# From the fifth block on, three quarters of the second layer in high and low parts, read from the PSUM banks, and the table of late blocks made earlier

## The chip, the cores and the metric

The kernel runs on one core of one Trainium2 chip, in one launch. The metric is device time in microseconds (us) of that core, the median of several executions. TensorE is called PE here, VectorE DVE, ScalarE ACT, GpSimd POOL and SyncE SP.

## The reference

```python
x = x + cross_attention(ctx_1024, layernorm(x))     # 32 batches, 128 context and 128 latent rows, 16 heads of 64
x = x + ffn(layernorm(x))

def ffn(x):                                          # 4096 tokens, E = 8 experts, D = 256, F = 1024
    assign = argmax(x @ centroids.T, axis=1)         # one expert for each token
    xn = normalise(x) * ln_g[e] + ln_b[e]
    h  = relu(xn @ w1[e].T + b1[e])                  # first layer, 256 -> 1024
    y  = x + h @ w2[e].T + b2[e]                     # second layer, 1024 -> 256
    a  = sigmoid(x @ centroids[e])
    return a * y + (1 - a) * x
```

Everything is float32 at the interface.

## The kernel before, in words

**Attention first, then blocks.** The first three quarters of the program are the attention: 64 steps over 16 pairs of batches. Each batch's finished rows are scattered by POOL into a table in HBM, `sorted_rows`, by expert. The feed-forward works on that table in blocks ("slots") of 256 rows of one expert. There are at most 23 slots; which expert and which rows a slot has is computed on DVE and read by SP as a register. The first six (`n_early` = 6) are placed before the last batches are ranked, by `early_blocks`; the others by `late_blocks` (line 1600), which also computes how many slots stay empty. From slot 16 on each engine branches around slots that are empty. In this input slots 0 to 18 run.

**Numbers in two parts.** PE multiplies plain float32 in two recorded passes, and the reduced format fp32r in one. To keep the accuracy with fp32r a number is split: `hi` is the number rounded to fp32r, `lo` the rest, and a product is made of three matmuls, `PASSES = ((0, 0), (0, 1), (1, 0))` (line 31). The first layer of slots 1 and up is wholly in parts (`layer_1`, line 888, matmuls on line 902). The second layer has 8 chunks of 128 hidden units (`FC` = 8). Of these `FS` = 4 go in parts (`in_parts`, line 929, matmuls on line 932) and 4 plain (`plain`, line 936, matmuls on line 938), for each of the two halves of 128 rows.

**One slot, engine by engine.** PE runs `layer_1(s + 1)`, then `layer_2_split(s)`. The first layer fills PSUM banks 0 to 3, two chunks each.

- ACT: `relu_parts(s + 1)` (line 1226) reads each bank and writes the first four chunks to `hid_raw` in SBUF (the tile `y_t`) and the last four to `hid_plain` (the tile `prob_t`); then `row_gain_bias(s + 2)` (1190, instruction 1208), `high_weights_2(s + 1)` (1244, instruction 1251), and at the head of the next slot `normalise_rows` (1172, instruction 1186) and `high_weights_1` (1164, instruction 1170).
- DVE: `low_weights_1(s + 2)` (instruction 1635), `split_hidden(s + 1)` (1638, instructions 1644 and 1645, once for each bank of two chunks in parts), `split_xn(s + 2)` (1622, instructions 1629 and 1631), `transpose_rows(s + 3)` (instruction 1620), `finish(s)` (1647, instructions 1658 and 1663 twice). `then_next` (1362) makes the next DVE instruction wait for a semaphore that the one before raises.
- POOL: `add_base(s + 2)` (two of instruction 1891), `low_weights_2(s + 1)` (1895, one instruction on line 1898 over 1024 elements), `write_rows(s)` (1903), an indirect DMA for each half.
- SP: the loads of the slots to come, in an order written out by hand (lines 652 to 670): `load_vectors`, `load_rows`, `load_weights_1`, `load_weights_2`, `load_b2`, and `move_rows`.

**What waits for what.** `layer_1(s)` waits for `f_xd` (`split_xn(s)` done), for `f_wl` (`low_weights_1(s)` done), and for each bank `i` until ACT has read it out two slots before (`f_ha`, line 894). `layer_2_split(s)` waits for `f_w2h`, `f_w2l` (the parts of its weights) and `f_hl` (the parts of its hidden units). The tiles of the feed-forward lie over tiles of the attention: `hid_hi` over `v_n`, `hid_lo` over `prob`, `w2_hl` in `head_out` and `w_o`.

**The hand-over.** Around slots 1 to 5 the order is written out line by line. On DVE (lines 1766 to 1791) it ends with `places` of the last two batches, `low_weights_1(4)`, `split_hidden(3)`, `split_xn(4)`, `late_blocks()`, `finish(2)`. On SP (lines 652 to 665) `load_weights_2(5)` and `load_b2(5)` come before the wait for the table and the first loads of slots 6 and 7.

## Time and profile before

| | |
|---|---|
| median of 3 runs | 1053.27 us (1052.5 to 1053.7) |
| the profiled execution | 1052.73 us |
| its span | 1050.9 us |
| granted clock of PE | 0.999 |
| PE busy | 1041.6 us, 99% |
| DVE, ACT, POOL busy | 844.9, 688.7 and 565.3 us |
| the feed-forward slots | from about 800 us to the end |

The span runs from the first recorded instruction to the last; the rest of the profiled time, 1.8 us, lies around it. All times of instructions are counted from the span's start. The chain is the sequence of work that ended last, followed back from the last instruction; a piece of it is counted from the end of the piece before.

### The profile page before, as it was taken

The page shows a single profiled execution, that of the slowest core. Times are in us where ns is not written, and L with a number is a line of the kernel's source. Part 1 is how long each engine was busy: PE and PEld are TensorE (multiplying, and loading weights), DVE is VectorE, ACT ScalarE, POOL GpSimd, SP SyncE. Part 2 cuts the span into 40 slices and gives each one's busy share as a digit, 9 for nine tenths or more (in the row PEclk, how much of TensorE's full clock was granted, in tenths as well). Part 3 has the DMA queues.
Part 4 walks back from the last instruction along what each step waited for, and adds up shares of the span by engine and source line. Part 5 has one row for each costly group of instructions (what it writes and reads, how often), then busy time and mean ns, then how long its engine had stood idle before and what let it go on. Part 6 is the DMA issues. An engine that isn't in the chain of part 4 may idle for free.

```text
span 1050.9 us, 24670 instructions
## 1 busy us (share of the span) xinstructions
PE 1041.6 (99%) x8610; PEld 940.5 (89%) x8610; DVE 844.9 (80%) x1979; ACT 688.7 (66%) x1838; POOL 565.3 (54%) x665
## 2 busy tenths in 40 slices
PE   9999999999999999999999999999999999999997
PEld 7889898988888888889898989889888999999997
DVE  7878888878888888888888879888887797767663
ACT  6765757675666767666757575766566666676761
POOL 1744464646454555545464646465444667566663
PEclk9999999999999999999999999999999999999999
DMA  6665657585757576767667585856356868777760
GB/s 212 160 169 148 170 156 189 146 215 142 201 146 197 142 193 155 200 156 197 159 168 185 142 210 137 213 144 171 91 153 196 307 198 294 250 234 234 249 194 31
DMA packets 159666, 190.57 MB, mean 181 GB/s; under 512 B 17454, under 2 KB 149038, under 8 KB 154673
## 3 DMA queue, kind: packets, MB, share of 16 engines
q1 hardware_dynamic: 155088, 179.09, 62.4%
q0 software_dynamic: 3360, 8.53, 2.2%
q8 instruction: 72, 1.18, 0.4%
q10 hardware_dynamic: 1088, 1.31, 0.4%
q14 instruction: 58, 0.47, 0.1%
HBM read 65.72 MB, written 46.07 MB: 106 GB/s over the span
## 4 chain that ended last, share of the span: by engine, by line
PE 96%; DVE 2%; POOL 1%; ACT 1%; DMA 0%; issue 0%; POOLq 0%; DVEq 0%
PE psum L742 17%; PE psum L775 16%; PE psum L812 11%; PE psum L902 10%; PE psum L791 10%; PE psum L827 9%; PE psum L761 8%; PE psum L938 6%; PE psum L932 5%; PE psum L830 1%; PE psum L883 1%; PE psum L914 1%; DVE neg_max L1410 1%; DMA c_in<-in_ctx_in 0%; PE psum L856 0%; DVE w_lo L1545 0%
## 5 line engine op out<-in xcount | busy, mean ns | idle before, releaser
L1823 POOL TENSOR_TENSOR prob<-prob,inv_sum 128x512 f32<-128x512 f32 x172 | 177.7, 1047 | 190.1 <-DVE inv_sum L1416 189.2
L1133 ACT ACTIVATE prob<-psum,neg_max 128x256 f32<-128x256 f32 x344 | 160.2, 478 | 38.8 <-DVE neg_max L1410 38.5
L1410 DVE TENSOR_REDUCE neg_max<-psum 128x2 f32<-128x512 f32 x256 | 161.9, 672 | 27.7 <-PE psum L791 27.5
L1422 DVE STREAM_TRANSPOSE prob<-prob 128x512 f32<-128x512 f32 x172 | 118.5, 698 | 12.3 <-POOL prob L1823 11.9
L1823 POOL TENSOR_TENSOR w_ring<-w_ring,inv_sum 128x512 f32<-128x512 f32 x76 | 78.1, 1041 | 76.0 <-DVE inv_sum L1416 75.7
L1140 ACT ACTIVATE head_out_hi<-psum 128x512 fp32r<-128x512 f32 x52 | 31.1, 597 | 105.6 <-PE psum L812 102.4
L1119 ACT ACTIVATE v_n<-psum 128x512 f32<-128x512 f32 x128 | 77.9, 608 | 26.7 <-PE psum L775 22.7
L1108 ACT ACTIVATE k_hi<-psum 128x512 fp32r<-128x512 f32 x128 | 77.0, 603 | 22.0 <-PE psum L742 21.3
L1461 DVE TENSOR_TENSOR k_lo<-psum,k_hi 128x512 fp32r<-128x512 f32 x128 | 85.7, 674 | 0.0
L742 PE MATMUL psum<-kv_t_hi,w_hi 128*128 128x512 f32 x252 | 85.0, 419 | 0.0
L775 PE MATMUL psum<-w_hi,kv_t_hi 128*128 128x512 f32 x256 | 80.2, 395 | 0.4 <-DVE k_lo L1461 0.4
L1133 ACT ACTIVATE w_ring<-psum,neg_max 128x256 f32<-128x256 f32 x152 | 70.7, 477 | 14.6 <-DVE neg_max L1410 14.6
L791 PE MATMUL psum<-k_hi,q_hi 64*128 64x256 f32 x512 | 79.1, 305 | 0.8 <-DVE q_lo L1468 0.7
L775 PE MATMUL psum<-w_lo,kv_t_hi 128*128 128x512 f32 x256 | 79.4, 391 | 0.0
L775 PE MATMUL psum<-w_hi,kv_t_lo 128*128 128x512 f32 x256 | 79.3, 391 | 0.0
L742 PE MATMUL psum<-kv_t_lo,w_hi 128*128 128x512 f32 x252 | 78.1, 391 | 0.0
L742 PE MATMUL psum<-kv_t_hi,w_lo 128*128 128x512 f32 x252 | 77.9, 390 | 0.0
L1133 ACT ACTIVATION_READ_ACCUMULATOR prob<-psum,neg_max 128x1 f32 x344 | 72.5, 211 | 0.0
L791 PE MATMUL psum<-k_lo,q_hi 64*128 64x256 f32 x512 | 72.5, 279 | 0.0
L791 PE MATMUL psum<-k_hi,q_lo 64*128 64x256 f32 x512 | 72.3, 278 | 0.0
L938 PE MATMUL psum<-w,prob_t 128*128 128x256 f32 x288 | 65.3, 379 | 0.0
L812 PE MATMUL psum<-w_ring,v_n 128*64 128x128 f32 x1024 | 63.0, 276 | 0.3 <-DVE cent_sum L1501 0.3
(215 smaller groups left out, 2952.4 us busy)
## 6 DMA issues: line engine op xcount, KB each, us to landing
sorted_rows<-filler SPq DMA_DIRECT2D x54, 660.0 KB
prob_t<-prob SPq DMA_DIRECT2D x172, 128.0 KB, 2.8
w_ring<-prob SPq DMA_DIRECT2D x172, 128.0 KB, 2.7
w<-in_experts SPq DMA_DIRECT2D x19, 1024.0 KB, 7.8
w_ring<-in_experts SPq DMA_DIRECT2D x18, 1024.0 KB, 6.7
prob_t<-w_ring SPq DMA_DIRECT2D x76, 128.0 KB, 2.8
w_ring<-w_ring SPq DMA_DIRECT2D x76, 128.0 KB, 2.7
w_ring<-normed SPq DMA_DIRECT2D x56, 128.0 KB, 3.0
```

Source lines behind the costliest of these rows:

```text
L742: last = pe.matmul(bank.rearrange("p (b t) -> p b t", b=2), k_w[hw][:, c, col:col + P], kv_t[hx][:, c, slot:slot + 2, :], start=(n == 0 an ...
L775: last = pe.matmul(bank, kv_t[hx][:, c, slot, side * P:(side + 1) * P], v_w[hw][:, c, col:col + BANK], start=(n == 0 and c == 0), stop=(n ...
L791: ins = pe.matmul(psum[:, 2 * bb + parity, i * 2 * P:(i + 1) * 2 * P], q_s[hq][rows, u % 2, i, bb * P:(bb + 1) * P], k_s[hk][rows, u % 2, ...
L812: last = pe.matmul(bank[rows, (2 * bb + i) * P:(2 * bb + i + 1) * P].rearrange("p (a q) -> p a q", a=4), v_n[:, h % 2, bb, side, head * DH ...
L827: pe.matmul(bank[:, 0:d_model + n_experts], heads, w_o[hw][:, c, :], start=(n == 0 and c == 0), stop=False)
L902: last = pe.matmul(dst, w1_hl[hw][s % NW][:, c, f * P:(f + 1) * P], xn_hl[hx][:, s % 2, c, :], start=(n == 0 and c == 0), stop=(n == 2 and ...
L938: last = pe.matmul(bank, hid_plain[:, s % 2, f - FS, i * P:(i + 1) * P], w2_ring[s % NW2][:, f * d_model:(f + 1) * d_model], start=(first ...
L1133: act.activation(prob_at(u, bb)[:, :, parity, i], scores_i, ACT.Exp, bias=neg_max[:, at, i:i + 1], accum_out=prob_sum[:, at, i:i + 1]).the ...
L1410: dve.tensor_reduce(neg_max[:, (4 * u + n) % 8, :], psum[:, n, :].rearrange("p (i j) -> p i j", i=2), AXIS_X, ALU.max, negate=True).then_i ...
L1422: dve.transpose(probs, probs).then_inc(s_quad, 1)
L1461: last_reads(item, dve.tensor_tensor(k_s[1][:, u % 2, i, :], work_bank(number[item]), k_s[0][:, u % 2, i, :], ALU.subtract))
L1823: pool.tensor_tensor(probs, probs, inverse, ALU.mult).then_inc(s_soft, 1)
```

## The change

From slot 4 (`FIRST_MORE`) on, the second layer takes 6 of its 8 chunks in parts and 2 plain; slots 1 to 3 stay at 4 and 4. For these slots ACT writes the ReLU of the chunks back to the PSUM bank that it read (`hidden_raw`), and DVE splits it out of the bank, three banks for a slot. `layer_1` therefore waits for banks 0 to 2 until DVE has split them (`f_hl`), for bank 3 still for ACT. ACT no longer waits for `f_hl` in these slots. `hid_hi` and `hid_lo` get 8 chunks for each of two slots (over `v_n`, and over `prob` and `prob_t`), and the plain chunks now lie in the place of `hid_hi` that belongs to their number. ACT's `high_weights_2` covers 1536 elements in place of 1024, and POOL's `low_weights_2` becomes three instructions of 512 elements. On DVE `late_blocks()` goes ahead of `low_weights_1(4)`, and `split_xn(4)` ahead of `split_hidden(3)`. On SP `load_weights_2(5)` and `load_b2(5)` go behind the wait for the table, the rows and vectors of slot 6, the rows of slot 7 and the first-layer weights of slot 6.

```diff
+FIRST_MORE = 4
-            FS = FC // 2
+            SPLIT_EARLY, SPLIT = FC // 2, 3 * FC // 4
-                hid_hi = sbuf(late, "hid_hi", [P, 2, FS, BLOCK], F32R)
-                sbuf(late, "hid_between", [P, 3 * FS * BLOCK])
-                hid_lo = sbuf(late, "hid_lo", [P, 2, FS, BLOCK], F32R)
+                hid_hi = sbuf(late, "hid_hi", [P, 2, FC, BLOCK], F32R)
+                sbuf(late, "hid_between", [P, FC // 2 * BLOCK])
+                hid_lo = sbuf(late, "hid_lo", [P, 2, FC, BLOCK], F32R)
+            def hidden_raw(s, i):
+                return psum[:, i, :] if s >= FIRST_MORE else hid_raw[:, i, :]
+            def n_split(s):
+                return SPLIT if s >= FIRST_MORE else SPLIT_EARLY
+            def hidden_split(s):
+                return sum(n_split(t) // 2 for t in range(FIRST_SPLIT, s + 1))
 # SP
-                load_weights_2(n_early - 1)
-                load_b2(n_early - 1)
                 scattered(n_batches)
                 run = block_steps(sp, count_empty(sp))
                 run(n_early, (load_rows,), (load_vectors,))
                 run(n_early + 1, (load_rows,))
                 run(n_early, (load_weights_1,))
+                load_weights_2(n_early - 1)
+                load_b2(n_early - 1)
                 run(n_early + 1, (load_weights_1,))
 # PE, layer_1
+                        elif s > FIRST_MORE and i < SPLIT // 2:
+                            pe.wait_ge(f_hl, hidden_split(s - 2) + i + 1)
                         else:
                             pe.wait_ge(f_ha, FC // 2 * (s - 2) + i + 1)
 # PE, layer_2_split
-                        pe.wait_ge(f_hl, FS // 2 * (s - FIRST_SPLIT + 1))
+                        pe.wait_ge(f_hl, hidden_split(s))
-                            for f in range(FS):
+                            for f in range(split):
-                        for f in range(FS, FC):
+                        for f in range(split, FC):
 # ACT, relu_parts
-                        if i < FS // 2 and s > FIRST_SPLIT:
-                            act.wait_ge(f_hl, FS // 2 * (s - 1 - FIRST_SPLIT) + i + 1)
-                        elif i == FS // 2 and s >= 2:
+                        if i < split // 2 and FIRST_SPLIT < s < FIRST_MORE:
+                            act.wait_ge(f_hl, hidden_split(s - 1) - SPLIT_EARLY // 2 + i + 1)
+                        elif i == split // 2 and s >= 2:
                             wait_made(act, ("fy", s - 2, 1))
-                            dst = hid_raw[:, i, at] if f < FS else hid_plain[:, s % 2, f - FS, :]
+                            dst = hid_plain[:, s % 2, f - SPLIT_EARLY, :] if f >= split else hidden_raw(s, i)[:, at]
 # DVE
                 def split_hidden(s):
-                    for i in range(FS // 2):
+                    for i in range(n_split(s) // 2):
 ...
-                        then_next(dve.tensor_copy(hi, hid_raw[:, i, :]))
-                        dve.tensor_tensor(lo, hid_raw[:, i, :], hi, ALU.subtract).then_inc(f_hl, 1)
+                        raw = hidden_raw(s, i)
+                        then_next(dve.tensor_copy(hi, raw))
+                        dve.tensor_tensor(lo, raw, hi, ALU.subtract).then_inc(f_hl, 1)
 ...
                 places(n_batches - 1)
+                late_blocks()
                 low_weights_1(4)
+                split_xn(4)
                 split_hidden(3)
-                split_xn(4)
-                late_blocks()
                 finish(2)
 # POOL
                 def low_weights_2(s):
                     pool.wait_ge(f_w2h, s - FIRST_SPLIT + 1)
-                    raw = w2_ring[s % NW2][:, 0:FS * d_model].rearrange("p (f d) -> p f d", f=FS)
-                    pool.tensor_tensor(w2_hl[s % 2][1], raw, w2_hl[s % 2][0], ALU.subtract).then_inc(f_w2l, 1)
+                    raw = w2_ring[s % NW2][:].rearrange("p (f d) -> p f d", f=FC)
+                    hi, lo = w2_hl[s % 2]
+                    piece = 2 if s >= FIRST_MORE else SPLIT_EARLY
+                    for f in range(0, n_split(s), piece):
+                        last = pool.tensor_tensor(lo[:, f:f + piece], raw[:, f:f + piece], hi[:, f:f + piece], ALU.subtract)
+                    last.then_inc(f_w2l, 1)
```

## Rows read from the trace of the kernel before

**Rows 1.** The page, part 4: the chain that ended last, by engine.
```profile
PE 96%; DVE 2%; POOL 1%; ACT 1%; DMA 0%; issue 0%; POOLq 0%; DVEq 0%
```

**Rows 2.** The chain in order of time: start us, us, what, instructions.
```profile
857.15 5.76 PE psum L902 x48
...
869.66 5.76 PE psum L902 x48
...
876.86 3.46 PE psum L938 x16
...
881.75 5.76 PE psum L902 x48
...
1032.55 1.44 PE psum L932 x12
```

**Rows 3.** Lines 938 and 902 alone: count, durations ns min/median/max, first and last start us.
```profile
L938 PE MATMUL psum<-w,prob_t x288: 376/379/382, 837.5 to 1043.4; 128*128 128x256 f32 x144
L902 PE MATMUL psum<-k_hi,w_hi x288: 282/283/386, 818.3 to 1031.8; 128*128 128x256 f32 x144
```

**Rows 4.** Timeline of one late slot: start us, us, engine, line, [idle before].
```profile
931.00 2.28 DVE L1635 TENSOR_TENSOR w_lo<-w_ring,w_hi 128x2048 fp32r<-128x2048 f32 x1
...
937.61 1.05 ACT L1251 ACTIVATE head_out_hi<-w 128x1024 fp32r<-128x1024 f32 x1
937.74 0.43 DVE L1629 CAST k_hi<-c_in 128x512 fp32r<-128x512 f32 x1 [1.91 <-ACT c_in L1208]
938.20 0.69 DVE L1631 TENSOR_TENSOR k_lo<-c_in,k_hi 128x512 fp32r<-128x512 f32 x1
...
938.74 2.40 POOL L1898 TENSOR_TENSOR head_out_lo<-w,head_out_hi 128x1024 fp32r<-128x1024 f32 x1 [2.48 <-ACT head_out_hi L1251]
...
940.18 0.71 DVE L1620 STREAM_TRANSPOSE normed<-normed 128x512 f32<-128x512 f32 x1 [1.29 <-ACT normed L1186]
...
943.66 0.84 ACT L1241 ACTIVATE y_t<-psum,vec_ring 128x256 f32<-128x256 f32 x2 [1.70 <-PE psum L902]
```

**Rows 5.** Groups and single lines that price the changed instructions.
```profile
L1461 DVE TENSOR_TENSOR k_lo<-psum,k_hi 128x512 fp32r<-128x512 f32 x128 | 85.7, 674 | 0.0
...
L1644 DVE CAST hid_hi<-y_t x36: 410/419/671, 825.6 to 1030.6; 128x512 fp32r<-128x512 f32 x36
...
L1881 POOL TENSOR_TENSOR w_o_lo<-w_ring,w_o_hi x4: 1282/1292/1299, 41.7 to 54.3; 128x512 fp32r<-128x512 f32 x4
```

**Rows 6.** Timeline: DVE instructions that start beside a POOL instruction, twice.
```profile
27.78 3.02 POOL L1823 TENSOR_TENSOR prob<-prob,inv_sum 128x512 f32<-128x512 f32 x2 [0.87 <-DVE inv_sum L1416]
...
28.27 1.62 DVE L1545 TENSOR_TENSOR w_lo<-r_ring,w_hi 128x1024 fp32r<-128x1024 f32 x1
...
843.17 2.36 POOL L1898 TENSOR_TENSOR head_out_lo<-w,head_out_hi 128x1024 fp32r<-128x1024 f32 x1 [2.91 <-ACT head_out_hi L1251]
843.37 2.45 DVE L1663 SCALAR_TENSOR_TENSOR x_in<-x_in,r_ring,base 128x256 f32<-128x256 f32 x1
```

**Rows 7.** Timeline of the hand-over: the table of late blocks, and slot 5's preparation.
```profile
848.08 2.28 DVE L1635 TENSOR_TENSOR w_lo<-w_ring,w_hi 128x2048 fp32r<-128x2048 f32 x1
...
853.71 0.15 DVE L1561 COPY small<-psum 128x8 f32<-128x8 f32 x1
...
854.71 1.92 DVE L1604 TENSOR_TENSOR small<-small,taken 128x8 f32<-128x8 f32 x1
...
859.50 0.14 DVE L1614 CAST empty_i<-small 1x1 int32<-1x1 f32 x1
...
861.83 2.29 DVE L1635 TENSOR_TENSOR w_lo<-w_ring,w_hi 128x2048 fp32r<-128x2048 f32 x1
...
866.41 1.60 POOL L1891 TENSOR_SCALAR base<-r_more 128x256 f32<-128x256 f32 x2
```

**Rows 8.** Timeline of the last slot's weights.
```profile
1033.32 1.06 ACT L1251 ACTIVATE head_out_hi<-w 128x1024 fp32r<-128x1024 f32 x1
...
1034.46 2.35 POOL L1898 TENSOR_TENSOR head_out_lo<-w,head_out_hi 128x1024 fp32r<-128x1024 f32 x1 [4.90 <-ACT head_out_hi L1251]
```

More of the change, by code:

```diff
@@ L320, in build @@
             hid_raw = y_t[:].rearrange("p c b t -> p c (b t)")
-            hid_plain = prob_t_even[:].rearrange("p b a h i s q -> p b (a h i s q)").rearrange("p s (f t) -> p s f t", f=FC - FS)
-            w2_hl = [[w[:].rearrange(rule)[:, 0:FS * d_model].rearrange("p (f d) -> p f d", f=FS) for w in pair] for pair, rule in
+            hid_plain = v_n[:].rearrange("p s a b n -> p s (a b n)")[:, :, SPLIT_EARLY * BLOCK:].rearrange(
+                "p s (f t) -> p s f t", f=FC - SPLIT_EARLY)
+            w2_hl = [[w[:].rearrange(rule)[:, 0:FC * d_model].rearrange("p (f d) -> p f d", f=FC) for w in pair] for pair, rule in
                      ((head_out, "p b c t -> p (b c t)"), (w_o, "p c n -> p (c n)"))]
@@ L919, in layer_2_split @@
                 def layer_2_split(s):
+                    split = n_split(s)
                     pe.wait_ge(f_w2[s % NW2], 16 * (s // NW2 + 1))
@@ L926, in wait_parts, with in_parts @@
                         pe.wait_ge(f_w2l, s - FIRST_SPLIT + 1)
-                        pe.wait_ge(f_hl, FS // 2 * (s - FIRST_SPLIT + 1))
-                    def in_parts(bank, i, first):
+                        pe.wait_ge(f_hl, hidden_split(s))
+                    def in_parts(bank, i, first, last):
                         for n, (hw, hx) in enumerate(PASSES):
-                            for f in range(FS):
-                                last = pe.matmul(bank, hid_hl[hx][:, s % 2, f, i * P:(i + 1) * P], w2_hl[s % 2][hw][:, f, :],
-                                                 start=(first and n == 0 and f == 0), stop=(not first and n == 2 and f == FS - 1))
-                        return last
+                            for f in range(split):
+                                ins = pe.matmul(bank, hid_hl[hx][:, s % 2, f, i * P:(i + 1) * P], w2_hl[s % 2][hw][:, f, :],
+                                                start=(first and n == 0 and f == 0), stop=(last and n == 2 and f == split - 1))
+                        return ins
                     def plain(bank, i, first):
-                        for f in range(FS, FC):
-                            last = pe.matmul(bank, hid_plain[:, s % 2, f - FS, i * P:(i + 1) * P],
+                        for f in range(split, FC):
+                            last = pe.matmul(bank, hid_plain[:, s % 2, f - SPLIT_EARLY, i * P:(i + 1) * P],
                                              w2_ring[s % NW2][:, f * d_model:(f + 1) * d_model],
-                                             start=(first and f == FS), stop=(not first and f == FC - 1))
+                                             start=(first and f == split), stop=(not first and f == FC - 1))
                         return last
@@ L946, in layer_2_split @@
                         wait_parts(s)
-                        in_parts(bank, 0, False).then_inc(f_y, 1)
+                        in_parts(bank, 0, False, True).then_inc(f_y, 1)
                         bank = begin(("fy", s, 1))[:, 0:d_model]
-                        in_parts(bank, 1, True)
+                        in_parts(bank, 1, True, False)
                         plain(bank, 1, False).then_inc(f_y, 1)
@@ L952, in layer_2_split @@
                     wait_parts(s)
-                    in_parts(bank, 0, True)
+                    in_parts(bank, 0, True, False)
                     plain(bank, 0, False).then_inc(f_y, 1)
@@ L956, in layer_2_split @@
                     plain(bank, 1, True)
-                    in_parts(bank, 1, False).then_inc(f_y, 1)
+                    in_parts(bank, 1, False, True).then_inc(f_y, 1)
                 pe.wait_ge(s_blank, 1)
@@ L1226, in relu_parts @@
                 def relu_parts(s):
+                    split = n_split(s)
                     b1 = vec_ring[:, s % NR, 2 * KC:]
@@ L1250, in high_weights_2 @@
                         wait_made(act, ("fy", s - 2, 1))
[L1251 to L1252 removed]
+                    act.activation(w2_hl[s % 2][0][:, 0:n_split(s)], w2_ring[s % NW2][:, 0:n_split(s) * d_model]
+                                   .rearrange("p (f d) -> p f d", f=n_split(s)), ACT.Copy).then_inc(f_w2h, 1)
                 act.dma_start(c_in[:, 0:2, :], ctx_in[0:2].rearrange("b p d -> p b d")).then_inc(s_in[0], 16)
```

2 lines of the change are left out of this document (removed).

## The prediction, made before the changed kernel was run

> **What bounds the kernel now.** I read the chain first. 96% of it is PE [rows 1], so only two things can move the time: the work of PE itself, and a wait that comes to stand on it. Then the chain in order of time: from 857 us to the end it is one slot after another, and every start is the end of the one before. A slot is a first layer (48 matmuls, 5.76 us), a second layer in parts (two groups of 12), and between them the plain matmuls; from one first layer to the next it is 881.75 - 869.66 = 12.09 us [rows 2]. PE never waits there. Third I read the timeline of a late slot, to see how much room the other engines have [rows 4], and last the places where the order is not yet regular: the hand-over to the late slots [rows 7] and the last slot [rows 8].
>
> **The matmuls.** 16 plain records take 3.46 us, 0.216 each; 12 matmuls in parts take 1.44 us, 0.120 each [rows 2]. The change takes 8 plain records (1.73 us) out of a slot and puts in 12 in parts (2 halves, 2 chunks, 3 passes: 1.44 us). It saves 0.29 to 0.30 us. There are 16 plain records for each split slot and 288 in all [rows 3], so slots 1 to 18 run; 15 of them are from slot 4 on: 15 x 0.296 = **4.4 us saved**. A slot becomes 11.79 us long.
>
> **ACT.** The weights' high part grows from 1024 to 1536 elements: 1.05 us [rows 4] becomes at least 1.05 and in proportion 1.58; I take 1.5. ACT stands idle 1.70 us in each slot before its first ReLU [rows 4]; that hides it. If the cover were gone, 0.45 us a slot would delay the ReLUs, and next the splits. Writing the ReLU to PSUM in place of SBUF has no row. Nearest is the same ReLU to SBUF, 0.84 for two; it could be shorter or longer by some 0.1, also under that cover. I take it unchanged.
>
> **DVE.** Splitting out of the bank: the cast from SBUF takes 0.42 (an operand in SBUF, the same operation), a subtraction that reads 512 elements of PSUM 0.67 (the same source) [rows 5]. These are the bounds of the new cast; I take 0.67, because half the elements' time can hardly be lost by a subtraction that reads the same bank. The Trainium skill ("VectorE: DVE Perf Modes", section on why PSUM operands drop a tier) says that fp32 out of PSUM runs at the basic rate; by that rule it is the 0.67, and by the rate of the SBUF cast the sum would come out as in the first rival. A bank then costs 0.67 + 0.67 less the overlap, about 1.30 us, and a slot has three: 3.9 us where two took about 2.4.
>
> **POOL.** One subtraction of 1024 elements, 2.40 us [rows 4], becomes three of 512. POOL has done such a one: 1.29 us [rows 5]. So 3.9 us, 1.5 more.
>
> **Where POOL and DVE meet.** A DVE instruction with two operands in SBUF that starts beside POOL's subtraction does not run beside it: it ended 0.29 us behind it (843.37 + 2.45 against 843.17 + 2.36) [rows 6]. With two POOL instructions back to back DVE came between them: the pair took 3.02 us, and DVE's 1.62 ended at 29.89, before the second did at 30.80 [rows 6]. A transpose ran beside POOL undisturbed, 0.71 us [rows 4]. So a DVE step meets at most one piece each time it has to begin anew, 1.29 us. [...] The splits out of PSUM then wait for nothing, but the cast and the subtraction of `split_xn` do.
>
> **The regular slots.** Counted from the start of the first layer (929.9): DVE's low weights start at 1.1 now [rows 4]. `finish` of the slot before can meet up to two pieces, so 2.1 to 2.6; +2.2, +3.9: `split_xn` starts at 8.2 to 8.7 and ends 1.1 later, at the latest 9.9. It is due at 11.8. POOL's pieces start when ACT's weights are done, at 9.3, and end at 13.2; the second layer wants them at 17.5. PE's new wait for the bank: the third split is done at 8.7, the bank wanted at 14.7. Queued behind it on PE is the whole first layer, and the room is 6 us. **Nothing lost**, 1.9 us to spare.
>
> **The hand-over.** Here the room is less. The table took 853.71 to 859.64, 5.9 us, of which 1.75 was one small subtraction held up by POOL [rows 7]. Moved up it starts at 848.1 and ends at 852.3; `low_weights_1(4)` (2.28) ends at 854.6, `split_xn(4)` (1.15) at 855.7. The first layer of slot 4 is counted from 857.15 and must be released some 0.3 earlier, one matmul's 0.28 [rows 2, 3]: just in time. If POOL's 2.4 us subtraction for slot 3 falls in the gap of `split_xn(4)`, it ends at 858.1, and PE loses 1.2. `split_hidden(3)` and `finish(2)` follow, and `low_weights_1(5)` starts where it did, 861.83. The splits of slot 4 start at 864.0 and end at 867.9; there `split_xn(5)` now starts. POOL ends `add_base(5)` at 868.0 [rows 7], or up to 0.4 earlier, as less is in its way, and starts its three pieces: they collide. If the cast waits for the first piece and the subtraction for the second: 868.0 + 1.29 + 0.4 + 1.29 + 0.55 = 871.5. Due is 869.4 (869.66 less 0.3 [rows 2, 3]): 2.1 late. If the cast gets ahead and only the subtraction waits, 870.2: 0.8 late. If neither meets a piece, 869.0: nothing. Together the hand-over costs 0 to 2.5 us; I take **1.7**. What comes after is later by as much, and slot 6 has room again. The moved loads on SP: the rows and first weights of slot 6 are issued some 5 us sooner (seven issues with their register loads), `load_weights_2(5)` and `load_b2(5)` a few us later; their users come 15 us after. I cost them at nothing; without the cover it would be one load, some 7 us.
>
> **The end.** The last slot has no first layer behind it. Its second layer is due 6.03 us after 1032.55, less 0.3, on the clock of before at 1038.3. ACT's weights end at 1033.32 + 1.5 = 1034.8, POOL's three pieces at 1038.7, and with one `finish` between them at 1039.1 [rows 8, 5]. PE waits 0.4 to 0.9 us; I take **0.8**. Ends: nothing, and 1.5 if every piece meets DVE.
>
> **The sum.** -4.4 + 1.7 + 0.8 = -1.9 us. Against the profiled execution's own time, 1052.73, that is 1050.8; it stands 0.5 below the median, so for the median 1053.27 - 1.9 = **1051.4**, say 1051.3. A measurement of this kernel can tell about 0.2%, 2.1 us, from no change: the forecast lies just within that. Its own range is -1.0 to -2.9, 1050.4 to 1052.3.
>
> **Rivals.**
> First, the collision at the hand-over doesn't happen: the cast out of PSUM is faster (at 0.42 the splits end 0.75 us sooner, ahead of POOL), or POOL starts later. For it: the two meet within 0.3 us. Against: 0.67 is the better price. Then -4.4 + 0 to 0.4 + 0.4 to 0.8: 1049.1 to 1050.1.
> Second, slower: DVE and POOL hold each other up in every late slot. The place is `split_xn`. If `finish` slips to 3.3 us after the start of the slot, the cast arrives when POOL's first piece has begun (9.4); it then waits until 10.7, the subtraction for the second piece until 12.3, and ends at 12.9 in place of 11.8: 1.1 us for each slot. That is the point from which it decides. In 13 slots 14 us: 1053.3 - 1.9 + 14 = 1065; in every third, 1056. For it: a cycle of DVE and POOL (three pieces, `finish`, 2.2, 3.9, 1.1) adds up to about 11.8, the length of the slot. Against: POOL's start hangs on ACT, not on DVE, so the cycle is not closed.
> Third, the change saves PE nothing, because what it saves in the second layer is waited for elsewhere in the slot. Every margin I find is above 1 us, against 0.3 saved. 1053.3.
>
> **The numbers.** Forecast 0.60: of this 0.22 is beyond 0.2% (below 1051.2), 0.38 within. First rival 0.25, all faster. Second 0.12: 0.10 slower, 0.02 within. Third 0.03, within. Faster 0.47, same 0.43, slower 0.10. The range reaches down to the first rival with the end's cost nearly gone, 1048.9, and up to 1054.5, where the hand-over and the end cost their most and one slot in five slips; left out are most of the second rival and a gain above 4.4.
>
> **What would show it.** Right: from slot 6 on the chain's period is 11.79 us, with two groups of 18 matmuls in parts and 8 plain records between; POOL's subtraction of 512 elements at 1.29; DVE's cast out of psum at 0.67; a gap of 0 to 2 us on PE before the first layer of slot 4 or 5, released by DVE's `split_xn`, and one of 0.4 to 0.9 before the last second layer, released by POOL. Wrong: a period above 11.9 (second rival), no gap at the hand-over (first), a matmul in parts above 0.12 us, or ACT late with its first ReLU.

## The result, and the profile after

The changed kernel takes 1055.47 us (median of 21 executions, 1051.72 to 1057.99), the kernel before 1053.25 in the same comparison (1052.5 to 1055.03). The ratio is 1.0015, with a 95% interval of 1.0008 to 1.0022: 1.6 us slower, 0.8 to 2.3 (2.2 by the medians alone). The forecast was 1051.3, in a range up to 1054.5. The first thing to see is the spread: 6 us where the kernel before has 2.5. The second is that the loss is small beside it: a later set of 11 executions of the same kernel gave no loss ("The changed kernel again", below). So what follows explains why the forecast gain did not come; that the kernel is slower is less sure.

The profiled execution took 1055.55 us with a span of 1053.8, 2.9 above the span before. PE is busy less than before, 1038.5 us against 1041.6, so the saving is there, and more than all of it is lost in waits and what follows them. The page of after, parts 1 and 4:

```profile
PE 1038.5 (99%) x8670; PEld 940.0 (89%) x8670; DVE 876.5 (83%) x2009; ACT 694.0 (66%) x1838; POOL 582.0 (55%) x695
...
PE 93%; DVE 2%; POOL 2%; issue 1%; ACT 1%; DMA 0%; POOLq 0%; DVEq 0%; ACTq 0%
```

PE has fallen from 96% of the chain [rows 1] to 93%. What it waited for in the slots, from the waits of after (what ended the wait, us in total, times, longest):

```profile
PE psum L949 <- POOL w_o_lo L1921: 2.6, 1, 2.6
...
PE psum L918 <- issue: 1.0, 1, 1.0
...
PE psum L949 <- POOL head_out_lo L1921: 0.5, 1, 0.5
```

Lines 918, 949 and 955 are what 902, 932 and 938 were before: first layer, parts, plain. The chain of after in order of time (start us, us, what) puts these waits in their places:

```profile
857.09 1.05 issue
858.14 5.98 PE psum L918 x48
...
870.87 5.88 PE psum L918 x48
876.75 2.16 PE psum L949 x18
878.91 1.73 PE psum L955 x8
880.64 2.15 PE psum L949 x18
...
894.60 5.78 PE psum L918 x48
...
907.75 2.46 POOL base L1910
...
910.75 3.73 POOL w_o_lo L1921 x3
914.47 0.24 issue
914.72 2.95 PE psum L949 x18
917.66 2.77 PE psum L955 x8
920.44 2.15 PE psum L949 x18
922.58 5.76 PE psum L918 x48
...
934.38 5.76 PE psum L918 x48
...
1041.06 2.39 PE psum L949 x18
```

The regular slot is as forecast: 934.38 - 922.58 = 11.80 us, two groups of 18 in parts and 8 plain matmuls. Against it stand three places. The first layer of slot 4 is 1.05 us late: the moved `split_xn(4)` starts beside POOL's subtraction for slot 3, its cast (0.42 us alone) ends 0.28 us behind that subtraction, and the first layer starts when the rest of `split_xn(4)` is done at 858.04. The two lines, of POOL and of DVE:

```profile
853.16 3.87 POOL L1921 TENSOR_TENSOR w_o_lo<-w,w_o_hi 128x1024 fp32r<-128x1024 f32 x1 [0.54 <-ACT w_o_hi L1269]
854.70 2.61 DVE L1647 CAST k_hi<-c_in 128x512 fp32r<-128x512 f32 x1
```

The second layer of slot 7 was due at 912.2 (the first layer of slot 7 starts at 894.60; behind it come 5.78, a second layer of 6.04 and a first of 5.76) and starts at 914.72. The last second layer is some 0.5 late. And the matmuls behind the wait at slot 7 are slow: 2.95 where 2.16 is usual, 2.77 where 1.73 is. The stretches of after say why (stretch, its length, then busy time and count of PE, its weight loads, DVE, ACT and POOL, then PE's granted clock, the DMA engines' busy share and GB/s):

```profile
906.50:912.00 5.50, 5.50 (x48) 5.45 (x46) 5.39 (x8) 2.82 (x7) 4.25 (x4) 1.00 0.58 172
912.20:914.70 2.50, 0.00 (x0) 0.02 (x1) 2.19 (x4) 2.50 (x5) 2.26 (x2) 1.00 0.85 270
914.70:916.00 1.30, 1.28 (x11) 1.30 (x12) 0.74 (x2) 1.30 (x2) 0.63 (x1) 1.00 0.95 372
916.00:917.00 1.00, 1.00 (x8) 1.00 (x7) 0.12 (x1) 1.00 (x3) 0.69 (x2) 0.62 0.99 418
917.00:918.00 1.00, 1.00 (x6) 0.91 (x5) 0.59 (x1) 1.00 (x1) 0.96 (x2) 0.50 1.04 426
...
919.00:920.00 1.00, 1.00 (x4) 0.80 (x4) 0.42 (x1) 0.00 (x0) 1.00 (x2) 0.68 0.85 287
```

PE was fully busy, then idle for 2.5 us, and 1.3 us after it began again its clock went from 2.4 to 1.2 GHz for some 3 us. In this execution the wait is paid nearly twice.

The account of the profiled execution from the first layer of slot 4 to the end of the last second layer: -15 x 0.296 = -4.4 saved; slot 4 +1.05 and +0.3 for first layers of 5.98 and 5.88 in place of 5.76; slot 7 +2.5 of wait and +1.8 of half clock; the end +0.5 of wait and +0.2 in the matmuls behind it. Sum +2.0. PE's last matmul ends at 1047.35 where it ended at 1045.21 before: +2.1. The other 0.8 of the span lies behind PE's last matmul, at the last output write.

Why is POOL late at slot 7? Its timeline of after, then of before (start us, us, instruction, [idle before]):

```profile
898.58 2.32 POOL L1927 DMA_INDIRECT out<-x_in,r_more  x1 [0.30 <-issue]
907.75 3.00 POOL L1910 TENSOR_SCALAR base<-r_ring 128x256 f32<-128x256 f32 x2 [6.84 <-DVE x_in L1682]
910.72 3.75 POOL L1921 TENSOR_TENSOR w_o_lo<-w,w_o_hi 128x512 fp32r<-128x512 f32 x3
```

```profile
896.24 2.32 POOL L1903 DMA_INDIRECT out<-x_in,r_more  x1 [0.30 <-issue]
903.18 1.09 POOL L1891 TENSOR_SCALAR base<-r_ring 128x256 f32<-128x256 f32 x2 [4.62 <-issue]
904.23 2.41 POOL L1898 TENSOR_TENSOR w_o_lo<-w,w_o_hi 128x1024 fp32r<-128x1024 f32 x1
```

Between the output write of slot 5 and the first late slot POOL stands idle for 4.6 us before and 6.8 after. The code has two instructions there, ahead of the first `late_block`: a semaphore wait and a drain of POOL. I call the pair the entry wait. The semaphore wait (`f_out[0]` at 96) asks for the rows of slots 0, 2 and 4, the last of them slot 4's, and it costs nothing: the drain behind it is recorded from 0.16 us after the start of slot 5's second DMA instruction. The idle time is the drain's, in before and in after (count, its duration in ns, its start in us):

```profile
L1964 POOLq DRAIN  x1: 6592/6592/6592, 896.4 to 896.4; - x1
```

```profile
L1988 POOLq DRAIN  x1: 8817/8817/8817, 898.7 to 898.7; - x1
```

The profile names DVE's `finish` as what ended the idle time in after, because it ended at 907.59. But `add_base(8)`, the instruction behind the idle time, needs only `finish(4)`, and the drain's own record ends at 907.56. What the drain waits for can be read from the DMA packets in the traces. In all eleven profiled executions that have the entry wait it ends 2.1 to 2.2 us after the last packet of slot 5's write. That packet ends 4.5 us after the start of the second DMA instruction in before (at 900.78) and 6.8 us after it in after (905.35).

In before the entry wait ended in time for a single subtraction of 2.4 us, with the weights' low part ready at 906.6 against a due time of 911.7. In after the write is 2.3 us later (the three pieces for slot 6 and the `finish` that met them are ahead of it), the wait 2.2 longer, `add_base` meets DVE's `low_weights_1` (3.00 in place of 1.09), and the subtractions last 3.75: ready at 914.47. Of the 2.5 us that PE waits, that meeting is 1.9; without it, by the same numbers, PE would have waited an estimated 0.6.

### The profile page after: what moved, and what is told of

It reads as the page before. It is cut to its first block, busy times and chain, and to the rows that moved or that the text cites. A ratio compares the mean times of both kernels' runs of the same rounds, so it can differ in the third digit from the quotient of the medians.

```text
span 1053.8 us, 24820 instructions
## 1 busy us (share of the span) xinstructions
PE 1038.5 (99%) x8670; PEld 940.0 (89%) x8670; DVE 876.5 (83%) x2009; ACT 694.0 (66%) x1838; POOL 582.0 (55%) x695
## 4 chain that ended last, share of the span: by engine, by line
PE 93%; DVE 2%; POOL 2%; issue 1%; ACT 1%; DMA 0%; POOLq 0%; DVEq 0%; ACTq 0%
PE psum L756 17%; PE psum L789 16%; PE psum L826 11%; PE psum L805 9%; PE psum L841 9%; PE psum L918 9%; PE psum L775 8%; PE psum L949 6%; PE psum L955 3%; PE psum L844 1%; PE psum L897 1%; PE psum L930 1%; DVE neg_max L1428 1%; DMA c_in<-in_ctx_in 0%; POOL w_o_lo L1921 0%
## 5 line engine op out<-in xcount | busy, mean ns | idle before, releaser
L1259 ACT ACTIVATE psum<-psum,vec_ring 128x256 f32<-128x256 f32 x90 | 36.5, 444 | 44.7 <-PE psum L918 44.0
```

## The experiments

Theory A: the loss lies in the entry wait and what follows from it, beside 1.05 us at slot 4 and some 1 at the end. Rivals: the moved table or loads are at fault; or POOL and DVE hold each other up everywhere. Four sets of runs, with 8 to 12 executions of each kernel. Each set has its own runs of the kernel before, and the ratio is to those: 1053.85 us for the kernels again, without the entry wait, table back and parts from slot 8; 1053.46 for the kernel before without the entry wait, plain first, the two moves and the table in the middle; 1053.21 for both edits together, SP's order back, one instruction and parts from slot 6; 1053.04 for the last three. Kernels of different sets are compared by these ratios.

**The changed kernel again.**

> The changed kernel once more, for a second trace. Theory A (the wait of POOL for its output writes on the way into the late slots): the time depends on how late slot 5's output lands, so the wait on PE before the second layer of slot 7 (2.6 us in the first trace, and 1.8 us of half clock behind it) is there again in another size, or is absent in a fast execution; the two fixed losses, about 1.2 us before the first layer of slot 4 and 0.5 to 0.8 before the last second layer, are the same in both traces. Theory B (POOL's longer subtractions alone make it late): the wait before slot 7 is the same 2.6 us within 0.3. Time by both 1053 to 1057, 1 to 3 us above before.

1054.03 us, 0.9995 (0.9986 to 1.0004). The interval doesn't overlap that of the first set (1.0008 to 1.0022), and the spread is 2.7 us where the kernel before has 3.1. So the loss of 1.6 us, and with it the wide spread, did not repeat; three close relatives of this kernel below gave 1.0010 to 1.0014. What holds in both sets is that the gain of 4.4 us is gone.

In this profiled execution POOL's idle before `add_base` was 5.40 and the second layer of slot 7 waited 1.3 us, with no half clock. The profile puts the wait down to DVE's `split_hidden(8)`, which this layer doesn't need; the layer starts 0.24 us after POOL's last piece ends, as in after. POOL's pieces took 6.01 us in place of 3.75, because DVE's `low_weights_1(9)` came in between:

```profile
907.81 6.01 POOL L1921 TENSOR_TENSOR w_o_lo<-w,w_o_hi 128x512 fp32r<-128x512 f32 x3
```

```profile
909.30 3.38 DVE L1653 TENSOR_TENSOR w_lo<-w_ring,w_hi 128x2048 fp32r<-128x2048 f32 x1
```

Without that meeting the low part would have been ready at 911.6, 1.2 us before the due time of 912.8 (an estimate from these rows). So the place is the same, the size differs from execution to execution, and most of it takes two things: a late end of the entry wait, and the meeting with `low_weights_1` that it leads to.

**Without the entry wait.**

```diff
-                pool.wait_ge(f_out[(n_early - 2) % 2], 32 * ((n_early - 2) // 2 + 1))
-                pool.drain()
```

> The changed kernel without POOL's wait for slot 4's output and its drain on entry to the late slots; the same pair stands in each late slot behind the subtractions anyway. Theory A: the wait of PE before the second layer of slot 7 is gone with its half clock, 4.4 us less than the profiled execution of the changed kernel, so about 1051, 2 to 2.5 us below before, and a narrower spread. Theory B (three subtractions are 1.5 us longer and POOL is late with or without the drain): the wait stays 2 us or more and the time stays above before. Theory C (the loss sits in the earlier order of DVE): no difference.

1052.82 us, 0.9987 (0.9978 to 0.9996). The wait at slot 7 is gone: POOL's pieces run at 903.80 to 908.2. They now meet `split_xn(8)`, and the chain has "906.53 0.66 issue" ahead of the first layer of slot 8. Theory A was right about the wait and wrong about the time and the spread: it said 1051 and narrower, the time is 1052.8 and the spread 3.5 us against 2.7 for the repeat. Its 4.4 us was taken from one execution with the half clock in it; the repeat, in the same set, is 1.2 us above this kernel by the medians and 0.8 by the ratios, and these two intervals overlap.

**The kernel before without the entry wait** (the same two lines out of it).

> The kernel before without the wait for slot 5's output and the drain in front of the late slots on POOL. Theory A: POOL had room there before the change (its work for slot 7 ended ahead of the due time by over 1 us), so nothing changes: 1053.9, within 0.5 us. Rival D (the drain costs the kernel before too): 0.5 to 1.5 us faster.

1053.21 us, 0.9997 (0.9988 to 1.0006). As theory A has it: the wait had cover before the change. (The expectation speaks of slot 5's output; the semaphore wait is for slot 4's, as above.) The same edit is worth nothing there. After the change it is worth about 1 us by the two kernels above, not clear of noise, and 2.3 us by the next pair; the traces show the wait at slot 7 with it and not without. Only with the change did it come onto the path.

**Plain matmuls first**: a late second layer does bank 0's plain matmuls ahead of its wait for the parts.

```diff
-                    in_parts(bank, 0, True, False)
-                    plain(bank, 0, False).then_inc(f_y, 1)
+                    plain(bank, 0, True)
+                    wait_parts(s)
+                    in_parts(bank, 0, False, True).then_inc(f_y, 1)
```

(and bank 1 in parts first, then plain)

> The changed kernel, but a late second layer begins with its 8 plain matmuls' first 4 (bank 0) and waits for the parts behind them, 0.87 us later (4 x 0.216). Theory A (the loss sits in the waits of the second layer for POOL at slot 7 and at the end, 1.3 to 2.6 us and 0.5 us): the end's wait of 0.5 us is gone and the next bank's plain matmuls are no longer behind it, slot 7's wait is 0.87 us shorter than without the edit (0.4 to 1.7 in place of 1.3 to 2.6); the time is 1.2 us below the repeat of the changed kernel (1054.03), 1052.8. The first layer of slot 4 stays 1.05 late. Theory B (the pieces on POOL cost elsewhere, by locks against DVE in every slot): no change, 1054.

1054.8 us, 1.0013 (1.0002 to 1.0024), 1051.45 to 1057.71. The wait at the end is gone and slot 7's is 1.17 us, and yet the time didn't fall. Its timeline shows the chain of events behind slot 7:

```profile
906.82 3.61 POOL L1910 TENSOR_SCALAR base<-r_ring 128x256 f32<-128x256 f32 x2 [5.42 <-issue]
910.40 3.76 POOL L1921 TENSOR_TENSOR w_o_lo<-w,w_o_hi 128x512 fp32r<-128x512 f32 x3
...
918.55 3.75 POOL L1921 TENSOR_TENSOR head_out_lo<-w,head_out_hi 128x512 fp32r<-128x512 f32 x3
...
928.92 3.75 POOL L1921 TENSOR_TENSOR w_o_lo<-w,w_o_hi 128x512 fp32r<-128x512 f32 x3
```

```profile
918.11 4.47 DVE L1682 SCALAR_TENSOR_TENSOR x_in<-x_in,r_ring,base 128x256 f32<-128x256 f32 x1
...
929.53 3.43 DVE L1647 CAST k_hi<-c_in 128x512 fp32r<-128x512 f32 x1
```

Because POOL is late at slot 7, its pieces for slot 8 fall on `finish` (4.47 us in place of 0.49); because `finish` is late, DVE's next `split_xn` falls on the pieces for slot 9 (cast of 3.43 in place of 0.42); and the first layer behind it starts 2.3 us late, at 933.79. (In the repeat above `finish` took 3.44 us in this place and the next cast 1.33, and PE didn't wait: the same start need not cost anything.) Note also that the cast ends with the last of three pieces. I come back to that.

**Both edits together: no entry wait, plain first.**

> The changed kernel with two edits: no entry wait and drain on POOL, and the plain matmuls of bank 0 first in a late second layer. Theory A: as the kernel without the entry wait (span 1050.4, time 1052.15 in its profiled execution), less the wait at the end (0.5 us and the handing over behind it): 1051.5 to 1052.3. The first layer of slot 4 is still 1.05 late and that of slot 8 0.7, because DVE's split_xn meets POOL there. No wait at the second layer of slot 7, and no cascade from it (a finish of 4.5 us, then a cast of 3.4 us). Theory F (the cascade comes without the drain too, since it is a matter of how DVE's and POOL's cycles fall): some executions 2 us longer, median 1053.5 or more.

1052.1 us, 0.9991 (0.9982 to 1.0000), 1051.22 to 1054.12. Beside the run above the entry wait alone is the difference: 2.3 us by the ratios, whose intervals don't overlap (the medians differ by 2.7, but are of two sets). No instruction of DVE in the late slots shows the 4.5 or the 3.4. What is left of waits on PE is 1.01 at slot 4 and 0.64 at slot 8.

**More parts only from slot 8 on** (`FIRST_MORE = 8`).

> The changed kernel with three quarters in parts from slot 8 on in place of slot 4, so that the hand-over and the entry into the late slots run with the old sizes; the moved table and loads stay. 11 slots save 0.296 each, 3.3 us. Theory A: the entry wait falls back to what before has (no wait on PE), so the loss is 1.2 (moved table) and 0.7 (end): 1.4 us below before, 1051.9. Theory B says the same wait moves to slot 8 or 9, where the longer subtractions start, and the time is above 1053.

1053.04 us, 0.9990 (0.9981 to 0.9999), 1052.32 to 1053.86. The time is 1.1 above theory A's 1051.9, and its chain has no wait at slot 8 or 9, as theory B had it. Of the difference 0.9 lies behind PE's last matmul, which theory A left out (6.6 us to the end of the span, 5.7 in before). The entry wait is in it, but POOL's work for slot 7 is one subtraction of 2.40 and PE doesn't wait there. The first layer of slot 4 is 1.05 late as in the others: that comes from the moved table, not from the parts.

**The two moves alone**, in the kernel before.

> The kernel before with the two moves alone (DVE: table ahead of low_weights_1(4), split_xn(4) ahead of split_hidden(3); SP: the second weights of slot 5 behind the loads of slot 6); no further parts. Theory A: the cast of split_xn(4) starts beside POOL's three-subtraction stretch for slot 3 and the first layer of slot 4 is 1.05 to 1.2 us late; nothing else: 1053.9 + 1.1 = 1055.0. The entry wait of POOL changes nothing here, since a slot's POOL work is ended 1.5 us sooner (2.40 in place of 3.9). Rival C (the moved loads delay the output write of slot 5, and so POOL's drain): drain of 7.5 to 8.8 us in place of 6.6, and the second layer of slot 7 waits 0 to 1 us also here.

1054.85 us, 1.0009 (1.0001 to 1.0018): 1.4 slower than 1053.46 by the medians, 0.9 by the ratio, 1.1 forecast. Its chain has "857.18 1.08 issue" ahead of the first layer of slot 4 and no other gap to the end.

**SP's order back** in the changed kernel.

> The changed kernel with the order of SP's loads of before. Rival C (the moved loads make POOL's entry drain longer): the drain is back at 6.6 us, from 7.4 to 8.8, and the time is 1 us lower, 1053. Theory A (the drain is later because POOL's pieces and the output write in front of it are, and its length varies by itself): no difference that can be told, 1054 to 1055.

1054.23 us, 1.0014 (1.0004 to 1.0024). The moved loads are not at fault: the second layer of slot 7 waits as before, and the drain is as long. The chain of this kernel shows it (POOLq is POOL's sequencer; line 1988 is the entry's drain):

```profile
899.44 8.89 POOLq L1988
...
911.34 3.72 POOL w_o_lo L1921 x3
...
915.31 2.38 PE psum L949 x18
917.69 1.73 PE psum L955 x8
```

Here PE waited 2.6 us as in after, and its granted clock stayed at 1.00: the matmuls behind it take 2.38 and 1.73. The same wait cost 1.8 us more in after. That is one source of the spread that the traces show.

**The table back** where it was on DVE.

> The changed kernel with DVE's old order (first-layer low weights of slot 4, hidden split of slot 3, its input split, then the table of late blocks); all else as changed. Theory A: it gives back the 1.2 us before the first layer of slot 4 and nothing else, as long as slot 6 is still loaded in time; the wait before slot 7 remains, and the time is about 1 us below the changed kernel. Theory C (the reorder is what costs): the time falls below before, to 1051 or less.

1056.55 us, 1.0020 (1.0011 to 1.0029). Both theories were wrong. Slot 4 is on time, but slot 5 is not:

```profile
869.38 3.72 POOL L1921 TENSOR_TENSOR head_out_lo<-w,head_out_hi 128x512 fp32r<-128x512 f32 x3
```

```profile
869.98 3.41 DVE L1647 CAST k_hi<-c_in 128x512 fp32r<-128x512 f32 x1
```

```profile
870.76 3.46 issue
874.22 8.63 PE psum L918 x48
```

With the table behind `low_weights_1(4)`, DVE is 1.9 us later at `split_xn(5)` (869.98 against 868.04), its cast waits for all three pieces, PE loses 3.46 us and then 2.87 more at half clock (8.63 against 5.76). So the move costs 1.05 at slot 4 and saves 6.3 at slot 5 in this execution. By the ratios of the set (1.0020 against 0.9995 for the repeat, and the intervals don't overlap) it saves 2.6 us in all, once there are more parts. What this kernel doesn't have is a wait at slot 7: its slots are later by then.

**Table in the middle, plain first, no entry wait** (DVE: `low_weights_1(4)`, `split_xn(4)`, `late_blocks`, `split_hidden(3)`, `finish(2)`).

> The changed kernel with three edits: no entry wait and drain on POOL, plain matmuls of bank 0 first in a late second layer, and DVE's order low_weights_1(4), split_xn(4), table, split_hidden(3), finish(2). Theory A: -4.4 saved; split_xn(4) now lies at 850.3 to 851.5, ahead of POOL's subtraction at 853.2, so the first layer of slot 4 is on time; no wait at slot 7; no wait at the end: 1053.9 - 4.4 = 1049.5 at best, 1050.5 if split_xn(5) or (8) meets a piece once. Theory E (the table, not the place of split_xn(4), decides: with the table behind it the splits of slot 4 meet POOL's pieces as in the kernel with the old order): the first layer of slot 5 is over 2 us late with half clock behind it, 1054 or more.

1056.74 us, 1.0028 (1.0018 to 1.0038). Theory E it was: slot 4 on time, the cast of `split_xn(5)` 3.39 us long, the first layer of slot 5 8.04 us long and 4.8 late (PE's idle time before it).

**POOL's pieces in one instruction** of 1536 elements.

```diff
-                    piece = 2 if s >= FIRST_MORE else SPLIT_EARLY
+                    piece = n_split(s)
```

> The changed kernel with POOL's subtraction for the second weights as one instruction of 1536 elements in the late slots, in place of three of 512. Theory G (pieces back to back hold DVE out like one long instruction: the casts of 3.4 us in the other runs): 3 x 1.25 becomes about 3.65, and the time is that of the repeat of the changed kernel within 0.5 us, 1054. Theory H (my step: a DVE instruction comes in between the pieces): split_xn waits for up to 3.6 where it waited 1.3, so slots 5 and 8 lose 1 to 2 us more each: 1056 or more.

1055.21 us, 1.0023 (1.0014 to 1.0032), the median of eleven executions; a twelfth took 2607.9 us and is left out. Between the theories: 1.0 above the kernel with SP's order back (1054.23, the same set), 0.9 by the ratios, and the intervals overlap. H asked for 1056 or more. So by the time alone neither theory is shown. The profile shows more: the cast of `split_xn(5)` takes 3.16 us where it took 0.94 in after, and the first layer of slot 5 is 1.14 late; at slot 9 3.15 us and 2.34 late. Pieces can let the cast in:

```profile
867.42 4.40 POOL L1921 TENSOR_TENSOR head_out_lo<-w,head_out_hi 128x512 fp32r<-128x512 f32 x3
```

```profile
868.04 0.94 DVE L1647 CAST k_hi<-c_in 128x512 fp32r<-128x512 f32 x1
869.01 1.66 DVE L1649 TENSOR_TENSOR k_lo<-c_in,k_hi 128x512 fp32r<-128x512 f32 x1
```

That is after, at slot 5. DVE's cast comes 0.62 us behind POOL's start and gets in between the pieces (0.94), the subtraction again (1.66), and POOL's three take 4.40. In the kernel with the table back the cast comes 0.60 behind POOL's start, waits for all three (3.41), and POOL's three take 3.72, one behind the other. Both happen. Over all kernels with three pieces the cast of `split_xn` met them 14 times: 11 times it got in behind the first piece (0.83 to 1.33 us), 3 times it waited for all three (3.39 to 3.43; once each in the kernels with the table back, the table in the middle and plain matmuls first). The single instruction was met twice and held it both times.

**POOL waits for split_xn** before its pieces (`pool.wait_ge(f_xd, 2 * (s + 2))`).

> The changed kernel with one wait more: POOL begins its pieces for the second layer of slot s+1 (from slot 4 on) only when DVE's split_xn of slot s+2 is done. Theory J (the loss beyond 1.1 + 0.5 us is split_xn held out by all three pieces): no cast of k_hi over 1 us from slot 5 on, no first layer late but slot 4's (its cast meets the subtraction for slot 3, which isn't gated); the wait at the second layer of slot 7 stays, since the entry drain does; time 1053.5, spread 3 us or less. Rival K (finish then is held instead, by 3.9 us in every slot, and DVE's cycle of 2.2 + 3.9 + 1.1 + 0.7 + 0.9 + 3.9 = 12.7 us is longer than PE's 11.80): period above 11.9 and the time 1060 or more.

1055.07 us, 1.0010 (0.9999 to 1.0022), 1051.22 to 1057.16. K fell: the period stays. J fell too: the time is 1.6 above its 1053.5 and the spread 5.9 us. `split_xn` was kept free, but the profiled execution has slot 7's wait of 2.6 us (POOL's pieces took 5.78 there, with DVE's `low_weights_1` in between), with the clock at 0.50 behind it, and a `finish` of 3.05.

**Can both kernels be beaten?** Three tries, all with plain first and the table where it was. From slot 6 on, without the entry wait:

> Three quarters in parts from slot 6 on in place of slot 4, the table of late blocks where it was before, no entry wait on POOL, plain matmuls of bank 0 first. The hand-over to slots 4 and 5 is then the kernel before's, with POOL's and DVE's work for them as before. Theory A: 13 slots x 0.296 = 3.85 saved and no wait at slots 4 and 5: 1053.5 - 3.85 = 1049.6; 1051 if split_xn meets POOL's pieces once or twice, as in slot 8. Rival: with the table late DVE is behind at slot 6, the casts meet three pieces, 2 to 3 us with half clock: 1053 or more.

1052.52 us, 1.0001 (0.9990 to 1.0013), 1050.61 to 1057.19: 1050.0 of span at its profile, waits of 0.1, 0.4 and 0.6, but a spread as wide as that of after. It is 2.9 above theory A's 1049.6; no gain is shown. From slot 8 on, with the entry wait and without:

> Three quarters in parts from slot 8 on, the table where it was before, plain matmuls of bank 0 first, entry wait on POOL kept. Hand-over and entry are then the kernel before's. Theory A: 11 slots x 0.296 = 3.26 saved, nothing lost at slots 4, 5 and 7 and at the end, and 0.75 us more behind the last matmul as in all kernels with more parts: 1053.3 - 3.26 + 0.75 = 1050.8, spread 2 us as for the kernel with parts from slot 8 on and the table early (1052.3 to 1053.9). Rival: the meeting in slot 8 or 9 comes as it did in slot 8 of others: 0.7 late, 1051.5, or with three pieces 2 to 3 late: 1053.5.

> As the kernel before it in this call, without the entry wait and drain on POOL. Theory A: the entry has room while slots 6 and 7 have two subtraction quarters only, so the same time within 0.5 us, 1050.8. Rival: without the wait POOL is further ahead at slot 8, so its pieces meet split_xn differently: 0.5 to 1 us either way.

1051.9 us, 0.9990 (0.9981 to 0.9999), 1050.65 to 1056.58, and **1051.6 us, 0.9988 (0.9979 to 0.9996)**, 1050.63 to 1053.32. By the ratio the second beats the kernel before by 1.3 us (0.4 to 2.2). It beats the changed kernel by 2.8 if that has the ratio of its first set and by 0.7 if that of the second; the two were not run in one set. In its profile PE waits for nothing in any slot. The medians are 1.1 and 0.8 above the 1050.8 expected, with one execution of 1056.58 against the "spread 2 us" of the first. The two kernels don't differ beyond noise: with parts from slot 8 the entry wait has cover, as in the kernel before. In the first PE waits once, 0.97 at slot 6.

## Why the prediction was wrong

- **Matmuls, -4.4**: right. The period is 11.80 against 11.79 forecast; 0.12 us for a matmul in parts.
- **ACT, DVE, POOL in the regular slots**: right. 1536 elements 1.47 us (1.5 forecast); ReLU into the bank 0.81 for two (0.84); the cast out of PSUM 0.68 (0.67 taken, 0.42 the other bound); a piece 1.30 (median). The Trainium skill ("VectorE: DVE Perf Modes", why PSUM operands drop a tier) gave that cast the basic rate, and the trace agrees: 0.68 us out of PSUM, 0.42 out of SBUF. The late part of after by lines:

```profile
L1663 DVE CAST hid_hi<-psum 128x512 fp32r<-128x512 f32 x30 | 20.5, 682 | 0.8 <-ACT psum L1259 0.8
...
L1682 DVE SCALAR_TENSOR_TENSOR x_in<-x_in,r_ring,base 128x256 f32<-128x256 f32 x16 | 16.3, 1021 | 1.1
```

  The second line is where POOL and DVE do meet in regular slots: `finish`, 1021 ns on the mean for some 490 undisturbed. It has cover, since the period stays 11.80.
- **Hand-over, +1.7**: the sum was near (1.05 of wait and 0.3 in two slower first layers), the split was not, so the nearness is luck. Of the two collisions named, the one at slot 4 came (0.99 to 1.08 us in every profile with the table ahead of `low_weights_1(4)`; "1.2" was forecast for the case that POOL's subtraction falls in the gap of `split_xn(4)`, and the chosen value left it out in favour of slot 5). The one at slot 5 came too, but the first layer there was itself due 1.2 us later by then and lost nothing.
- **The end, +0.8**: 0.5 of wait and 0.2 in the matmuls behind it. Right as far as it goes. Behind PE's last matmul came 0.8 us more, at the last output write; no term had that.
- **The step that failed is "Nothing lost", the term of nothing for the regular slots, with POOL's start put at "when ACT's weights are done".** It gave POOL's pieces an end at 13.2 against 17.5 in the slot's own time, 4.3 us of margin. That was worked out in a regular slot and carried to all of them. POOL passes one irregular place in between, the entry to the late slots, with its drain. There it starts not when ACT is done (903.6 in after) but at 907.75, its pieces end at 914.47, and PE starts 2.5 us late: with the half clock behind it 4.3 us, of the 4.8 us between the forecast's -1.9 and the span's +2.9. 4.6 us of that idle time were in the trace of before to be seen. By that trace alone: 903.18, later by 1.5 for the three pieces ahead of it, then 1.1 and 3.9, gives 909.7, 2 us before the due time; with the write 2.3 later, the drain 2.2 longer and a met `add_base` it became 914.5. I hadn't worked out even the first number, and it would not have been enough: the two last terms, the longer drain and the meeting of POOL's work with `low_weights_1`, are what turned 2 us of margin into a wait.
- **The size of a meeting.** "A DVE step meets at most one piece each time": in after it held at slot 5, and in three other kernels it was all three (3.4 us for a cast of 0.42). The Trainium skill ("SBUF — State Buffer", who interferes with whom) says that a VectorE instruction in a two-port mode contends with GpSimd for a shared pair of SBUF ports, and that whichever issues first has the pair for its whole instruction, while the other waits. The traces agree for one instruction: a held cast ends 0.28 us behind POOL's. That a row of instructions can hold the pair without a gap no row of before could show.
- **The half clock**, 1.8 us behind slot 7, wasn't in any term.
- **A small slip**: the first rival's lower end, by its own terms (1053.27 - 4.4 + 0.4), is 1049.3, not 1049.1. Nothing hangs on it.

The second rival ("DVE and POOL hold each other up in every late slot", with `split_xn` as the place) was right that such meetings can reach PE, and wrong in place and number. In after no first layer behind slot 4 is late for `split_xn`; in other kernels one or two are (3.5 and 4.8 us at slot 5 with the table back and in the middle, 0.7 at slot 8 without the entry wait, 2.3 at one slot with plain matmuls first and with the single instruction), and then it dies out. What PE waited for at slot 7 was POOL's own work, met by `low_weights_1`, which the rival doesn't name. It was given 0.12, at 14 us; that its "every third slot", 1056, lies near the measured time is luck.

What stays open: what makes the packets of slot 5's write end 4.1 to 6.9 us after its second DMA instruction starts, and so sets the idle time of 4.6 to 6.9 us; what decides whether DVE gets in between two pieces; why 2.6 us of idle time are followed by half clock in one execution and not in another; and why the changed kernel was 1.6 us slower in one set and not in the next. The last output write is a case of the first: from PE's last matmul to the end of the span it takes 5.7 us in the three kernels that have no more parts and 6.2 to 6.9 in all others, and again its last packets run later (2.1 us after the start of their DMA instruction against 2.5 to 3.2).

The spread is not explained either. With the entry wait and more parts at slot 7 it was 2.7 to 6.3 us in seven sets of executions (the changed kernel twice), 5.6 or more in four of them; without the entry wait and with more parts it was 2.1 to 3.5 in four kernels and 6.6 in the one with parts from slot 6 on. With the entry wait and parts from slot 8 it was 1.5 and 5.9. That speaks against one cause alone.

## What to carry to other kernels

A margin found in the regular slots holds for the regular slots. Walk each engine's own queue once through every place where the loop changes form, with the new durations, and put its waits for its own DMAs in the sum. A wait that costs nothing before a change (here 0 us in the kernel before) can be the first thing to cost when the work behind it grows by 1.5 us. And where a forecast gain is 4 us and PE is at 99%, a wait of 2 to 3 us on PE can cost nearly double, for the clock may fall behind it (it did in four of seven profiles here). Compare medians and spreads, not one profile, and repeat a difference of 0.15% in a second set before building on it: here it was 1.0015 and then 0.9995.

## What the hardware showed that was not expected

- With 2.5 to 4.8 us of idle PE the granted clock fell to 0.50, in the idle time or up to 1.3 us behind it, for 3 to 7 us (after, the table back, the table in the middle, the kernel in which POOL waits for `split_xn`), but not after a wait of 2.6 us in the kernel with SP's order back, nor after 2.3 us in the one with plain matmuls first and in the one with a single piece.
- Three POOL instructions of 1.25 us back to back held a DVE cast of 0.42 us for 3.4 us (3 of 14 meetings), or let it in behind the first of them (11 of 14, some 0.9 us), with the same offset of 0.6 us at the start.
- A drain of POOL behind an indirect DMA write ended 2.1 to 2.2 us after the last packet of that write, in eleven of eleven profiles: 6.6 us of drain before, 8.8 in after.
- POOL's indirect DMA instruction takes 0.97 to 1.02 us alone and 3.14 when it starts with DVE's subtraction of 2048 elements (861.83 to 864.12 [rows 7]), ending 0.9 us behind it, in the kernel before too. Started 0.8 us into such a subtraction it takes 2.32 and again ends 0.9 us behind it.

```profile
861.87 3.14 POOL L1903 DMA_INDIRECT out<-x_in,r_ring  x1 [5.26 <-DVE x_in L1663]
```
